# Eight unread matmuls among the scores of heads 5 and 6, and the fourth projection moved between the fourth step's scores

## The reference

```python
x = layernorm(x + attention_1(x))                 # conv, position, q/k/v, 16 heads of width 16, bf16 softmax
x = layernorm(x + attention_2(x, context))        # causal self-attention plus attention over 1024 context rows
x = layernorm(x + experts(x))                     # a table of 64 experts, one chosen per token by two argmax steps
# experts: cluster and tile scores -> gates -> argmax; h = gelu(x @ w1 + b1); comp = tanh(h @ w2 + b2)
#          hh = relu(comp @ spline_w1[tile] + b1[tile]); mag = hh @ spline_w2[tile] + b2[tile]
#          out = layernorm(x + mag * directions[tile] * scale) * gamma + beta
```

## Time and profile before

| | us |
|---|---|
| median of three runs | 2349.64 |
| lowest, highest | 2346.34, 2351.47 |
| profiled execution: its time | 2353.89 |
| profiled execution: its span | 2352.20 |
| TensorE busy | 2194.2 (93%) |
| VectorE busy | 1875.8 (80%) |
| ScalarE busy | 1382.4 (59%) |

### The profile page before, as it was taken

How to read it: one execution, slowest core, us unless ns; L and a number is a source line. 1 busy time by engine, 2 the same in 40 slices (tenths; PEclk the granted TensorE clock), 3 DMA queues, 4 the chain that set the end, 5 groups by cost and what they waited for, 6 DMA issues and landing times.

```text
span 2352.2 us, 37309 instructions
## 1 busy us (share of the span) xinstructions
PE 2194.2 (93%) x12927; PEld 1007.2 (43%) x12949; DVE 1875.8 (80%) x5149; ACT 1382.4 (59%) x2977; POOL 189.8 (8%) x349
## 2 busy tenths in 40 slices
PE   4899998999989999999999999999998999889992
PEld 1254434543345434454335543454334543345432
DVE  5858869788878879788787887979878786978844
ACT  2834677456854578446784457845676456844650
POOL 3011001000011000110001100010001100001000
PEclk7899999999999999999999999999999999989995
DMA  3600024000520006100160002500033000510000
GB/s 109 126 10 1 1 63 81 10 1 1 104 49 10 1 19 117 28 1 1 37 117 10 1 1 52 102 10 1 1 81 63 10 1 10 106 29 1 1 10 9
DMA packets 250844, 81.67 MB, mean 35 GB/s; under 512 B 236064, under 2 KB 247328, under 8 KB 250656
## 3 DMA queue, kind: packets, MB, share of 16 engines
q1 hardware_dynamic: 250656, 79.29, 16.4%
HBM read 16.35 MB, written 4.19 MB: 9 GB/s over the span
## 4 chain that ended last, share of the span: by engine, by line
PE 79%; DVE 9%; ACT 7%; issue 3%; DMA 1%; POOL 0%; SPq 0%; DVEq 0%; POOLq 0%; ACTq 0%
PE bank L1510 22%; PE bank L1563 13%; PE bank L1548 8%; PE bank L1205 7%; PE bank L1506 5%; PE bank L1467 5%; PE bank L1545 4%; ACT work L603 4%; DVE work L769 3%; PE bank L1330 3%; PE bank L1317 2%; PE bank L1523 2%; PE bank L1574 2%; PE bank L1296 1%; ACT work L659 1%
## 5 line engine op out<-in xcount | busy, mean ns | idle before, releaser
L659 ACT ACTIVATE work<-bank 128x512 f32<-128x512 f32 (+3 forms) x1536 | 737.8, 552 | 559.6 <-PE bank L1548 289.4
L1034 DVE TENSOR_REDUCE top_half<-bank 128x1 f32<-128x512 f32 x1024 | 625.6, 682 | 23.1 <-PE bank L1510 23.1
L1510 PE MATMUL bank<-k_c,q_c 32*128 32x512 f32 x2048 | 630.2, 636 | 0.0
L1548 PE MATMUL bank<-q_c,k_c 32*128 32x512 f32 x2048 | 549.0, 629 | 0.0
L603 ACT ACTIVATE work<-work,neg 128x512 bf16<-128x512 bf16 x512 | 362.7, 717 | 42.3 <-DVE work L769 42.3
L1510 PEld LDWEIGHTS bank<-k_c,q_c 32*128 32x128 f32 x2048 | 274.8, 185 | 244.3 <-DVE top_half L1034 159.8
L769 DVE TENSOR_SCALAR_CACHE_REDUCE work<-bank 128x512 bf16<-128x512 f32 x512 | 322.3, 686 | 49.0 <-PE bank L1301 32.4
L1563 PE MATMUL bank<-work,v_flat 128*32 128x512 f32 (+3 forms) x3072 | 320.1, 552 | 9.2 <-ACT work L659 8.8
L1031 DVE CUSTOM_DVE_ANT_0 masked<-bank,mask_w 128x384 bf16<-128x384 f32 (+3 forms) x512 | 223.3, 488 | 67.3 <-PE bank L1506 63.3
L1548 PEld LDWEIGHTS bank<-q_c,k_c 32*128 32x128 f32 x2048 | 227.0, 183 | 92.4 <-ACT work L659 57.2
L1545 PE MATMUL bank<-q_s,k_s 32*128 32x512 f32 (+3 forms) x1024 | 259.3, 476 | 0.0
(11 more groups left out here) (191 smaller groups left out, 2223.2 us busy)
## 6 DMA issues: line engine op xcount, KB each, us to landing
xT_pad<-xT SPq DMA_DIRECT2D x16, 256.0 KB, 3.4
ctx_sb<-ctxT SPq DMA_DIRECT2D x8, 512.0 KB, 3.3
x_res<-x SPq DMA_DIRECT2D x8, 512.0 KB, 4.7
out<-r_sb SPq DMA_DIRECT2D x8, 512.0 KB, 3.2
work<-work SPq DMA_TRANSPOSE x112, 4.4
qk_sb<-qkT SPq DMA_DIRECT2D x1, 512.0 KB, 4.6
pe_sb<-peT SPq DMA_DIRECT2D x1, 256.0 KB, 4.0
v_sb<-vT SPq DMA_DIRECT2D x1, 256.0 KB, 5.2
```

What stands on the lines that cost most here:

```text
L659: nc.scalar.activation(pT[:, s % PT_SLOTS, g, q0:S], exp_bank(n)[:, 0:S - q0], ACT.Exp, scale=SCALE).then_inc(pT_ready, 1)
L1034: nc.vector.tensor_reduce(top_half[:, i % 2, g, u // 2, u % 2:u % 2 + 1], scores, AX.X, ALU.max, negate=True).then_inc(slot_out, 1)
L1510: mm(dst, q_c[rows, i, P * t:P * (t + 1)], k_c[rows, i, S * half:S * (half + 1)], start=True, stop=True, tile_position=(GW * g, 0)).then_i ...
L1548: mm(dst, k_c[rows, i, P * u:P * (u + 1)], q_c[rows, i, :], start=True, stop=True, tile_position=(GW * g, 0)).then_inc(sT_mm, 1)
```

## The change

Three edits, all in `batch` of the tensor queue.

- `scores1` takes a bank `spare`; where it is given, one unread matmul (`keep_clock(spare, 1)`) stands ahead of each of the head's four scores, ahead of the score's own wait. It is given for heads 5 (bank 6) and 6 (bank 7) where `prev` is true.
- Ahead of head 5's scores stands a wait for `ln_stats[1]`, so that bank 6 is read; ahead of head 6's the wait for `qk_cast`, which stood after them, so that bank 7 is read.
- `unit(3)` moves from behind the gather to between the second and the third score of step 3, in all batches.

```diff
-                def scores1(h):
+                def scores1(h, spare=None):
                     i, rows = h // GH, slice(GW * (h % GH), GW * (h % GH + 1))
                     for t in range(NT):
                         n = NT * h + t
+                        if spare is not None:
+                            keep_clock(spare, 1)
                         pe.wait_ge(s1_evac, b * H * NT + n - A1_BANKS + 1)
...
                 for h in range(2, H):
-                    scores1(h)
+                    if prev and h == 5:
+                        pe.wait_ge(ln_stats[1], b * NT)
+                        scores1(h, 6)
+                    elif prev and h == 6:
+                        if ahead:
+                            pe.wait_ge(qk_cast, (b + 1) * NT + 1)
+                        scores1(h, 7)
+                    else:
+                        scores1(h)
...
                         if h == 6:
-                            if ahead:
-                                pe.wait_ge(qk_cast, (b + 1) * NT + 1)
                             route(c)
...
                     for r in range(GH):
                         scores(m, r)
+                        if m == 3 and r == 1:
+                            unit(3)
...
-                    if 3 <= m < 6:
+                    if 4 <= m < 6:
                         unit(m)
```

## The result

The changed kernel takes 2367.93 us, the median of four runs (2365.20 to 2369.42), beside 2350.55 for the kernel before on the same chip (2346.34 to 2352.43). The ratio is 1.0068, with a 95% interval of 1.0047 to 1.0089. It is slower by 0.7%, outside my range and on the other side of my forecast. The profiled execution took 2367.01 us with a span of 2365.2. That span is 13.0 us longer than the one of the prediction's sum (2352.2), and this is the number to be explained.

What follows compares the result with a forecast made beforehand. TensorE's in-order queue and its clock dips were taken as the bound. Terms +2.4 + 1.0 - 4.8 - 2.1 - 1.4 = -4.9; with half of batch 4's dip -2.5, so 2347.1 us from 2349.64; range 2335 to 2360.

Steps and rivals of the forecast that it cites:

- The move of projection 3: Between the fourth step's scores, batches 1 to 7: -0.3 us a batch, -2.1 in all, ends -0.7 and +1.9.
- Batch 4's dip: TensorE's fall to 1.2 GHz after ScalarE's featB copy in batch 4; fillers were to remove it: -4.8 us.
- The fillers' price: Eight fillers at heads 5 and 6, 0.24 us each: +0.4 us a batch, times six batches: +2.4.
- The other path: ScalarE's featB copy comes 0.97 us later, less 0.66 of idle: at most 0.3, beside TensorE's 0.4.
- batch 7's +1.0: Fillers in batch 7, already at 1.2 GHz there, fall partly into the wait for VectorE: between 0 and +2, taken +1.0.
- the warm sum: Batch 1's lead at full clock: spline starts 424.0, projection 5 about 429.6 instead of 430.28, -0.7 us.
- The clock in the new idle time: TensorE idle some 1.9 us before projection 4: +0.1 if projection 4 runs slow, +1.9 if projection 5 does too.
- Rival 2: Clock falls in the idle before projection 4, both last projections at 1.2 GHz: +12.9, or 2362.5 us; chance 0.2.
- Batch 0: No gather or spline there; scores and projection 3 take 4.2 us at full clock instead of 5.67: -1.4.
- The chances: Whole kernel against a 0.2% difference: faster 0.37, the same 0.41, slower 0.22.

## Why the prediction was wrong

Two steps of the sum failed. The fillers were priced at 0.4 us a batch and cost 1.7. The move of projection 3 was put at -0.3 us a batch, and the lead took +10.3 over the seven batches, by a new wait for VectorE, by projections 4 and 5 at 1.2 GHz around it, and in four batches by projection 3 at 1.2 GHz in part.

*Batch 4's dip: right, and partly luck.* I took the whole 4.8 for the profiled execution, and it came: 4.7, with 0.9 and 1.2 more in batches 2 and 6, where I hadn't seen anything. That it counts in full is owed to the execution of before, which has it. The profile of the move alone, without fillers, doesn't have it either.

*The fillers' price: the term was mis-sized, by a wrong row.* I priced a filler at 0.24 us from pv1's four, matmuls of one kind in a row. Among scores of another kind it takes 0.32, and so does each score behind it. The way of the sum was right. With 0.32 the transposes end 1.59 later, at 346.11, and head 6's last score starts 7 x 0.32 after that, at 348.35, or 1.76 later than 346.59; measured are 6.99 - 5.28 = 1.71. The other path, ScalarE's copy less its 0.66 us of idle time, gives 1.59 - 0.66 = 0.9, and with head 5's fillers alone it is 0.8. So six times 0.4 became six times 1.7, while batch 7's +1.0 came as forecast. Blocks cost 0.46, and none in batch 7; I priced the kernel with blocks.

*Projection 3: the warm sum was 0.4 to 0.7 too good.* I had the spline at 424.0 and projection 5 at 429.6, that is 79.3 and 84.9 us after the copy. The warm batches 3 and 4 of the move alone have 79.56 for the first, and 85.65 and 85.31 for the second. The first is close. The second failed at the scores of the sixth step: I let projection 5 start 5.6 us after the spline's start, and it took 6.1 and 5.75. What I didn't price at all is that splitting the step splits VectorE's work too: it takes two maxima, stands idle through projection 3, and takes the other two late. Ahead of all four scores the projection costs VectorE only one wait.

*The clock in the new idle time: the risk was named, and its value put too low.* Rival 2 was this, with 0.2 and 2362.5 us. Its mark was that projection 5 is slow in more than half of the batches, and that did not come: to the next row it takes 3.57 and 3.53 us in batches 1 and 3, 2.13 in batch 5, and 1.82, its warm time, in the others. The slow piece is mostly projection 4, with 3.56 to 3.68 us in batches 2, 4 and 5 and 3.50 in batch 7. Projection 3 itself, which I had warm, was still slow in batches 1, 3, 5 and 6 (2.81 to 3.18 us instead of 1.91). The place was right: the block in that idle time lifts the clock to 0.95 and more and brings the ratio from 1.0054 and 1.0068 to 1.0020. I put my value at -0.3, in the better half of -0.7 to +1.9, and held against the rival that dips ended after projection 3 in the trace of before. But there no idle time stood behind it. The lead cost +10.3 in place of -2.1, more than the 7 x 0.1 of one slow projection and less than the 13.3 of rival 2.

*Batch 0: wrong sign.* I forecast -1.4 from a full clock, and got +1.8. TensorE there:

```profile
145.84 1.98 PE L1475 MATMUL bank<-featB,wk_sb 128*128 128x512 f32 x4
...
149.81 1.10 PE L1514 MATMUL bank<-k_s,q_s 32*128 32x128 f32 x4 [0.94 <-DVE top_s L1031]
150.84 3.64 PE L1475 MATMUL bank<-featB,wcq_sb 128*128 128x512 f32 x4
```

Projection 3 is warm, in 1.98, as forecast. But TensorE then waits 0.94 us for VectorE, which was late by the split, and the fall comes at projection 4 instead (3.64; it took 2.00 before). A dip that I counted as won had only moved.

*The chances.* The parts that I named for "faster" add up to 0.38, and those for "the same" to 0.40, where I wrote 0.37 and 0.41. Nothing hangs on it.

*The rule weighed.* The Trainium skill, "TensorE: Matmul & The Clock Gate", section "Why this matters for your kernels", asks for no long idle gaps between bursts, and by it the fillers at heads 5 and 6 were needless. Batch 4's clock of 0.65 with 11.27 us of 12 busy, and 1.00 in all batches 1 to 6 of all fourteen profiles with fillers, speak against leaving it at that. In the lead the trace points the rule's way, since filling an idle time brought the clock back; but that idle time is 1.76 us, which isn't a long gap by that section.

*Still open.* The two parts don't add. The split move costs 0.3% alone, nothing beside head 6's block (0.9971 against 0.9968), and 0.57% beside both blocks (1.0008 against 0.9951). The table of ratios can't say why. The traces show where: over batches 1 to 7 the lead takes 332.1 us before, 333.5 with the move alone, 321.8 with fillers among the scores alone, and 342.4 and 340.7 with both. That the timing of the batches decides where the dips fall, and so how long the lead is, is argued, not shown.

## What to carry to other kernels

Price an unread matmul by rows in which it alternates with the same neighbours, or put it in a block: a block of four equal matmuls ran at 0.24 us each, the same ones among shallower ones at 0.32, and made the shallower ones 0.32 as well. Don't fill the same wait twice: what one head's fillers delayed, the next head's wait took up by half, until that wait had fillers of its own. When a piece of TensorE's work is moved to keep its clock, look at what the reading engine does with the group that it parts; put it ahead of the group, not inside, and fill the wait that it leaves elsewhere, where a block costs nothing. When a dip disappears from a stretch, look for it at the next wait before counting it as won.

## What was not expected of the hardware

A weight load of 32 rows behind a matmul of 128 rows, or the other way round, was not covered by that matmul: it stood in the open, with 0.23 us of idle time on the load queue before each. Behind one of its own kind it was covered. So a switch between kinds of matmul cost 0.1 us here, even between pv1 and the transposes, which are equally deep. At the lower clock a filler and a score take 1.07 us (2036.72 - 2035.65) instead of 0.64, as batch 7 of the changed kernel shows, TensorE, the fillers:

```profile
2035.65 0.61 PE L1355 MATMUL bank<-k,identb 128*128 128x512 bf16 x1
...
2036.72 0.61 PE L1355 MATMUL bank<-k,identb 128*128 128x512 bf16 x1
```

And the dips come and go between batches with one order of work: the lead of the changed kernel has 0.76, 0.92, 0.76, 0.91 and 0.66 in five batches in a row. The kernel before took from 2341.9 to 2367 us over 33 runs, more than most of the differences in this study; only ratios to runs on the same chip tell them apart.
